# A decoder's expert stage on one Trainium2 core: three blocks made one, rows weighed before the gather, results added up in DRAM by the scatters

## The reference

```python
N, D_MODEL, D_FF, N_EXPERTS, TOP_K = 2048, 256, 512, 8, 2
xn = _layernorm(x, ln_gamma, ln_beta)
xf = xn.reshape(-1, D)
logits = jnp.clip(xf @ router_w.T, -CLAMP, CLAMP)
probs = ...                                   # softmax over 8 experts, clipped
topk_p, topk_i = jax.lax.top_k(probs, TOP_K)
dense_gate = zeros((N, N_EXPERTS)).at[arange(N)[:, None], topk_i].add(topk_p)
for eid in range(N_EXPERTS):
    xe = xf * dense_gate[:, eid:eid + 1]      # the gate weighs the input row
    gu = xe @ gate_up_w[eid].T
    gate, up = jnp.split(gu, 2, axis=-1)
    hidden = jax.nn.silu(gate) * up
    out = out + hidden @ down_w[eid].T
return x + out
# and around it: x = _layernorm(x + that)     -> layernorm(2 x + out)
```

## Time and profile before

| what | us |
|---|---|
| median of 3 runs (lowest, highest) | 1420.37 (1419.14, 1420.39) |
| the profiled execution, its time | 1422.48 |
| the profiled execution, its span | 1420.8 |
| expert stage in it: block 1 | from about 1076 to 1145 |
| block 2 | from 1145 to 1388 |
| block 3 | from 1388 to the end |

### The profile page before, as it was taken

How to read it: one execution, slowest core, us unless ns; L and a number is a source line. 1 busy time by engine, 2 the same in 40 slices (tenths; PEclk the granted TensorE clock), 3 DMA queues, 4 the chain that set the end, 5 groups by cost and what they waited for, 6 DMA issues and landing times. The chain is left out here.

```text
span 1420.8 us, 25057 instructions
## 1 busy us (share of the span) xinstructions
PE 1197.0 (84%) x8059; PEld 873.5 (61%) x8060; DVE 881.0 (62%) x1545; ACT 743.3 (52%) x2046; POOL 608.3 (43%) x664
## 2 busy tenths in 40 slices
PE   7888589575999999999899999998984368999970
PEld 4544367454667767776666777665763357777750
DVE  2588799773445555563445566665886656677745
ACT  2598457334556556655555566652661035555532
POOL 1155457557436223322633322101664336666635
PEclk9999799797899999999999999999996569999995
DMA  9100000010010010001010001005401001111105
GB/s 303 27 1 0 0 1 2 1 30 16 16 30 16 16 30 16 16 1 31 15 25 17 5 16 45 1 1 224 133 1 45 23 19 49 44 48 48 48 33 178
DMA packets 36136, 56.04 MB, mean 39 GB/s; under 512 B 6528, under 2 KB 27392, under 8 KB 36032
## 3 DMA queue, kind: packets, MB, share of 16 engines
q1 hardware_dynamic: 32288, 44.47, 10.5%
q0 software_dynamic: 3744, 10.23, 2.2%
HBM read 34.90 MB, written 9.31 MB: 31 GB/s over the span
## 5 line engine op out<-in xcount | busy, mean ns | idle before, releaser
L2016 DVE TENSOR_REDUCE ga_neg_top<-ps 128x1 f32<-128x128 f32 (+7 forms) x256 | 181.9, 752 | 195.2 <-PE ps L1786 194.8
L1897 ACT ACTIVATE ga_e<-ps,ga_neg_top 128x128 f32<-128x128 f32 (+7 forms) x256 | 188.2, 743 | 7.5 <-DVE ga_neg_top L2016 6.8
L1906 ACT COPY ga_e_tr<-ps 128x512 f32<-128x512 f32 (+3 forms) x192 | 92.0, 479 | 174.6 <-PE ps L1795 172.1
L1795 PE MATMUL ps<-ident,ga_e 128*128 128x128 f32 x1152 | 165.1, 279 | 0.8 <-DVE ga_e_tr L2024 0.8
L1811 PE MATMUL ps<-ga_e_tr,ga_v 128*64 128x256 f32 x1152 | 151.7, 391 | 4.1 <-ACT ga_att L1914 4.1
L1795 PEld LDWEIGHTS ps<-ident,ga_e 128*128 128x128 f32 x1152 | 123.3, 142 | 28.0 <-ACT ga_e L1897 14.7
L2024 DVE COPY ga_e_tr<-ps 128x128 f32<-128x128 f32 (+3 forms) x192 | 105.8, 551 | 35.1 <-PE ps L1795 34.8
L2528 DVE TENSOR_TENSOR ex_w_lo<-ex_gate_up,ex_w_hi 128x1024 fp32r<-128x1024 f32 x78 | 92.7, 1229 | 42.1 <-ACT ex_w_hi L2493 42.0
L1971 POOL TENSOR_TENSOR ga_q_lo<-shared,ga_q_hi 128x1024 fp32r<-128x1024 f32 x15 | 35.5, 2370 | 175.5 <-ACT ga_q_hi L1887 175.5
L2493 ACT CAST ex_w_hi<-ex_gate_up 128x1024 fp32r x78 | 77.9, 1046 | 50.5 <-PEq L2189 35.0
L1811 PEld LDWEIGHTS ps<-ga_e_tr,ga_v 128*64 128x64 f32 x1152 | 72.4, 136 | 48.9 <-issue 23.3
(11 more groups left out here) (330 smaller groups left out, 2738.7 us busy)
## 6 DMA issues: line engine op xcount, KB each, us to landing
shared<-shared SPq DMA_DIRECT2D x80, 128.0 KB, 2.4
ex_gate_up<-in_ex_gate_up SPq DMA_DIRECT2D x1, 8192.0 KB, 24.3
ex_down<-in_ex_down SPq DMA_DIRECT2D x1, 4096.0 KB, 35.7
x_tr<-in_x_tr SPq DMA_DIRECT2D x4, 512.0 KB, 7.3
x_nat<-in_x SPq DMA_DIRECT2D x1, 2048.0 KB, 11.7
xn_rows<-x_tr SPq DMA_DIRECT2D x8, 256.0 KB, 2.1
x_tr<-choice_rows SPq DMA_DIRECT2D x8, 256.0 KB, 4.9
shared<-choice_rows SPq DMA_DIRECT2D x8, 256.0 KB, 5.5
```

The costliest lines, as they stand in the source:

```text
L1795: last = nc.tensor.transpose(ps_tr[n % 2][:, (kb - k0) * P:(kb - k0 + 1) * P], e[half][t % 2][:, kb * P:(kb + 1) * P], core.ident[:])
L1897: nc.scalar.activation(e[half][t % 2][:, 0:blocks(t) * P], ps_scores(t, half), ACT.Exp, bias=neg_top[t % 2][:, half:half + 1], accum_out=s ...
L1906: nc.scalar.copy(e_tr[g % 2][:, k0:k1, half, t % 2 * P:(t % 2 + 1) * P], ps_tr[n % 2][:, 0:(k1 - k0) * P].rearrange("p (k t) -> p k t", t= ...
L2016: nc.vector.tensor_reduce(neg_top[t % 2][:, half:half + 1], ps_scores(t, half), AX.X, ALU.max, negate=True).then_inc(top_ready, 1)
```

## The change

The three blocks become one, and four things change within it.

1. **Rows are weighed in advance.** As soon as a choice's gates are known, ACT multiplies all 16 tiles of `xn` with them (L2410 of the changed kernel, 32 activations of 128x256), and SP writes them to `gated_rows` (16 DMAs of 256 KB, a row for each choice). `xn_rows` goes. The loop's gather fetches by the choice's number straight into `row`; POOL's multiplication and the buffer `tokens_in` go. The gather of a tile waits until PE has transposed the tile before it.
2. **The slot table** needs two bf16 numbers a slot and no gates: no work on POOL, `at_place` has room for both choices, the running sum over experts takes 3 steps in place of 8, and the expert of each slot tile is worked out after the one-hots.
3. **The scatters add.** They have `compute_op=ALU.add` and go to `summed_rows`, which has one row for each token and is filled with 2x beforehand: ACT doubles x in 4 activations of 128x1024 and SP writes them in 5 DMAs. POOL waits for the scatter before, ahead of each.
4. **The last part** loads one tensor (8 DMAs of 256 KB), and neither POOL's nor DVE's addition is left. SP waits for the scatters itself.

The core of the diff:

```diff
+                for n in range(TILES // DOUBLED):
+                    tiles = slice(n * DOUBLED, (n + 1) * DOUBLED)
+                    sp.wait_ge(doubled_ready, n + 1)
+                    sp.dma_start(summed_rows[0:N, :].rearrange("(n p) d -> p n d", p=P)[:, tiles, :],
+                                 doubled[n // len(HALVES)][:, HALVES[n % len(HALVES)], :]).then_inc(summed_written, 16)
+                sp.dma_start(summed_rows[N:N + P, :], doubled[0][:, 0, :]).then_inc(summed_written, 16)
+                for i in range(2):
+                    for g in range(GROUPS_OF_TILES):
+                        tiles = slice(g * GROUP, (g + 1) * GROUP)
+                        sp.wait_ge(gated_ready, i * GROUPS_OF_TILES + g + 1)
+                        sp.dma_start(gated_rows[i * N:(i + 1) * N, :].rearrange("(n p) d -> p n d", p=P)[:, tiles, :],
+                                     gated[i][:, tiles, :]).then_inc(gated_written, 16)
+
+                sp.wait_ge(scattered, 16 * SLOT_TILES)
...
+        def fetch(pool, g):
+
+            nc.gpsimd.tensor_copy(tile_source[:], column(source, g)).then_inc(source_ready, 1)
+            pool.wait_ge(source_ready, g + 1)
+            apart(pool, core.pool_waited)
+            nc.gpsimd.indirect_dma_start(row, None, gated_rows,
+                                         bass.IndirectOffsetOnAxis(ap=tile_source[:], axis=0)).then_inc(gathered, 16)
...
+                pool.wait_ge(gated_written, 16 * 2 * GROUPS_OF_TILES)
+                pool.wait_ge(sources_ready, 1)
+                fetch(pool, 0)
+
+                def step(g, t, u1, u2, u3):
+                    if g is not None and not at(g, 0):
+                        need(pool, rows_tr_ready, g)
+                        apart(pool, core.pool_waited)
+                        fetch(pool, g)
+                    if u3 is not None:
+                        pool.wait_ge(down_copied, u3 + 1)
+                        apart(pool, core.pool_waited)
+                        nc.gpsimd.tensor_copy(tile_target[:], column(target, u3)).then_inc(target_ready, 1)
+                        pool.wait_ge(target_ready, u3 + 1)
+                        need(pool, scattered, 16 * u3)
+                        apart(pool, core.pool_waited)
+                        nc.gpsimd.indirect_dma_start(summed_rows, bass.IndirectOffsetOnAxis(ap=tile_target[:], axis=0),
+                                                     rows_out, None, compute_op=ALU.add).then_inc(scattered, 16)
...
+                for i in range(2):
+                    act.wait_ge(gates_ready, i + 1)
+                    for t in range(TILES):
+                        last = nc.scalar.activation(gated[i][:, t, :], xn[:, t, :], ACT.Copy, scale=gates[:, i, t:t + 1])
+                        if t % GROUP == GROUP - 1:
+                            last.then_inc(gated_ready, 1)
+
+                act.wait_ge(sources_ready, 1)
+                act.wait_ge(gated_written, 16 * 2 * GROUPS_OF_TILES)
+                act.wait_ge(summed_written, 16 * (TILES // DOUBLED + 1))
```

More of the change, by code:

```diff
@@ L2104, in stage_experts @@
     BATCHED = BANK // D
+    LEFT = EXPERTS // 2
+    CHOICE_PARTS = 2
+    DOUBLED = 4
+    HALVES = [slice(n, n + DOUBLED) for n in range(0, TILES // 2, DOUBLED)]
     GROUPS_OF_TILES = TILES // GROUP
@@ L2271, in _ @@
                 last.then_inc(ranks_ready, 1)
+                pe.wait_ge(choice_values_ready, 1)
                 for i in range(2):
                     pe.wait_ge(places_ready, i + 1)
[L2275 to L2279, removed]
@@ L2282, in _ @@
+                lagged(pe, SLOT_TILES, 2, step, turns=True)
             @block.scalar
             def _(act):
+                act.wait_ge(core.x_loaded, 16)
+                for n in range(TILES // DOUBLED):
+                    tiles = slice(n * DOUBLED, (n + 1) * DOUBLED)
+                    nc.scalar.activation(doubled[n // len(HALVES)][:, HALVES[n % len(HALVES)], :], core.x_nat[:, tiles, :], ACT.Copy,
+                                         scale=2.0).then_inc(doubled_ready, 1)
                 for n in range(TILES // BATCHED):
@@ L2292, in _ @@
+                lagged(act, SLOT_TILES, 2, step, turns=True)
+                for g in range(GROUPS_OF_TILES):
+                    act.wait_ge(offset_ready, g + 1)
+                    for t in range(g * GROUP, (g + 1) * GROUP):
+                        last = nc.scalar.activation(xn[:, t, :], xn[:, t, :], ACT.Identity, bias=offset[:, t:t + 1],
+                                                    scale=rstd[:, t:t + 1])
+                    last.then_inc(final_ready, 1)
             @block.vector
@@ L2344, in _ @@
-                for x in range(1, EXPERTS):
-                    link(nc.vector.tensor_tensor(ends[:, x:x + 1], ends[:, x - 1:x], count[:, x:x + 1], ALU.add))
-                link(nc.vector.tensor_tensor(starts[:], ends[:], count[:], ALU.subtract))
+                link(nc.vector.tensor_copy(count, count_int[:]))
+                for n, distance in enumerate((1, 2, 4)):
+                    summed = reach[n + 1][:, LEFT:] if n < 2 else ends[:]
+                    link(nc.vector.tensor_tensor(summed, reach[n][:, LEFT:], reach[n][:, LEFT - distance:LEFT - distance + EXPERTS], ALU.add))
@@ new lines, in _ @@
+                link(nc.vector.tensor_tensor(starts[:], ends[:], count, ALU.subtract))
+                link(nc.vector.scalar_tensor_tensor(work[:], starts[:].unsqueeze(1).to_broadcast(by_tile), float(P), ps_rank[:, 0:TILES, :],
+                                                    ALU.mult, ALU.add))
+                link(nc.vector.tensor_tensor(picks[:], picks[:], work[:].unsqueeze(1).to_broadcast([P, 2, TILES, EXPERTS]), ALU.mult))
+                link(nc.vector.reduce_sum(slots_f[:], picks[:], AX.X))
@@ L2349, in _ @@
+                for i in range(2):
+                    one_hot(at_place[:, i * TILES:(i + 1) * TILES, :], place_f[:, i, :], place_iota, P).then_inc(places_ready, 1)
                 by_slot = [P, SLOT_COLUMNS, EXPERTS]
@@ L2371, in _ @@
-                link(nc.vector.tensor_copy(gate_parts[:, 0].bitcast(F32R), gates[:]))
-                link(nc.vector.tensor_tensor(gate_parts[:, 1], gates[:], gate_parts[:, 0], ALU.subtract))
-                for i in range(2):
-                    last = one_hot(in_tile[:, i], tile_f[:, i, :], slot_iota, SLOT_COLUMNS)
-                last.then_inc(in_tile_ready, 1)
-                link(nc.vector.tensor_scalar(slots_part[:], slots[:], P - 1, None, ALU.bitwise_and))
-                link(nc.vector.tensor_copy(place_f[:], slots_part[:]))
```

351 lines of the change are left out of this document (144 added, 207 removed).

## The result

The changed kernel takes 1496.81 us (median of 4 runs, 1493.11 to 1498.83), the kernel before, run beside it, 1420.38 (1419.14 to 1425.89). The ratio is 1.0527, with a 95% interval from 1.0492 to 1.0562. The predicted time was 1389.0, the range 1379 to 1416. The profiled executions have spans of 1491.3 and 1420.8 us, so 70.5 us have to be found in the traces.

What follows compares the result with a forecast made beforehand. POOL's full turn, mean 5.57 us, was taken as the loop's bound, with PE close behind. Front -12.9, loop -4.2, scatter to load -6.7 and last part -8.0 sum to -31.8 against 1420.8, a median of about 1389; range 1379 to 1416.

Steps and rivals of the forecast that it cites:

- POOL in the loop: POOL's turn without multiplication and gap: 5.49 to 4.55 us, nothing late behind the gather's new wait, POOL no longer the bound.
- the rival for the slower side: Loop: an adding scatter that lands late holds ACT; at d = 2.8 a turn takes 7.4, time 1460; chance 0.16.
- POOL's own turn: Loop: POOL's work per turn, 5.49 us less 0.94 for the multiplication and its gap, 4.55.
- The front: From the count to PE's first transposes: shorter slot table chain of 15.5 us, weighed rows hidden with almost no cover; gain 12.9.
- The adding scatter: Loop's scatter chain: 4.6 us plus d; with d = 0.8 a turn of 5.4, together -4.2 us.
- d: Extra time of an adding scatter over a plain one, bounded by 0 and 2.8 us, taken as 0.8.
- max(5.2, 4.6 + d): Loop turn: the larger of PE's 5.2 us and the scatter chain's 4.6 + d; 5.4 at d = 0.8.
- The two ends: After the last scatter: SP's load sooner, 6.7; last part 24.5 us (bounds 21.5 and 24.5, by POOL's DRAIN) for 32.5, 8.0.
- a group's 1.5: Last part: eight groups at 1.5 us each, 12.0 in all, where a group took 2.78 before.
- A small d: Loop rival: d under 0.5, PE the bound at 5.2 a turn, time 1381; chance 0.26.
- late weighed rows: Front rival: the 16 writes to `gated_rows` end 13.7 us after the sources, front's gain gone, time 1403; chance 0.08.
- The second rival: Loop: scatter's extra between 1.2 and 1.7; at 1.4 a turn takes 6.0, time 1410; chance 0.10.

Runs made afterwards that it cites:

- experiment 1: Changed kernel with the scatter placed ahead of the gather in POOL's step, all waits kept: 1389.41 us, ratio to the kernel before 0.9778.
- experiment 2: Changed kernel, old order, with two buffers for gathered rows, so the gather waits for PE's transposes of the tile before the last: 1393.56 us, ratio 0.9793.
- experiment 3: Kernel before with only one wait added: POOL's gather waits for PE's transposes of the tile before. 1505.2 us, ratio 1.0573.
- experiment 6: Changed kernel with the scatter ahead of the gather and two buffers for finished rows and their indices: 1383.68 us, ratio 0.973.
- experiment 5: Changed kernel with the scatter ahead of the gather and scatters that overwrite in place of adding (addition in DRAM left out): 1378.69 us, ratio 0.9701.
- experiment 7: Changed kernel, gather still ahead of scatter, with two buffers for gathered rows and two for finished rows: 1380.79 us, ratio 0.9711.
- experiment 8: Changed kernel with the scatter ahead of the gather, plus a POOL drain right behind the last scatter: 1387.23 us, ratio 0.9752.
- experiment 4: Changed kernel, order and waits kept, with scatters that overwrite in place of adding: 1467.1 us, ratio 1.0317.

## Why the prediction was wrong

**The step that failed** is in *POOL in the loop*: "Behind the new wait at the gather (PE's transposes of the tile before) nothing is late: copy, gap and landing are 3.9 us, and the next transposes come a turn, 5.2 us, later." That was reckoned for the gather, and for the gather it is right: PE waits for gathered rows 6.1 us in the whole changed kernel. What stands behind the waiting instruction on POOL is the scatter, and it was not reckoned. In POOL's step the gather of tile g goes with the scatter of tile g - 4. The wait is for PE's transposes of g - 1; the results of g - 4 have come from PE in the turn before that, so the scatter could go about when that turn begins, and the transposes come near its end (after the gate/up matmuls). The prediction priced the scatter's delay behind the wait at nothing, without a reason. The trace has 6.83 us from the data to the issue, and `rows_out` is single, so this goes once round the cycle. Experiments 1, 2 and 3 show the cause from three sides: order mended, wait mended, wait added alone. The prediction named the single buffer of the gather in its last line as what could make it wrong, but gave it no price and no chance; the rival for the slower side was put on the landing.

**POOL's own turn** is a second step that failed, hidden by the first. The prediction took 0.94 off 5.49, got 4.55 and went on with "So POOL isn't the bound any more". Without the chain through `rows_out` POOL's turn is 5.33 us (experiment 6): the scatter holds it 1.67 us in place of 1.52, and the copy behind it takes 0.77 in place of 0.18.

**The front** was right and too small. The -12.9 was reckoned to PE's first transposes; to the first gather's issue the same terms give 1134.8 - 1146.8 = -12.0, against -15.5. The count was there at 1115.7, 2.4 us sooner than before, and the chain behind it took 14.3 us in place of 15.5. ACT's 32 activations ended at 1123.6 and not at 1130.7, so the cover was wider than reckoned. `gated_rows` was there in time: POOL was released by the sources (27.9 <-DVE ex_source above), not by the writes.

**The adding scatter** landed as sized: 3.8 us. The prediction built this from a plain 3.0 and d = 0.8. In experiment 5 a plain scatter lands after 2.4 (median) in a loop just as busy, with an issue of 1.0. Against that one the addition costs 1.4, of which 0.6 is the issue; why the kernel before had 3.0 and 1.52 is not shown. So the landing is right by luck in part: no row gave d, and d is 0.8 or 1.4 by the plain scatter it is held against. By the turn's term, max(5.2, 4.6 + d), a turn should take 5.4; experiment 1 has 5.54, and experiment 7, with the chain opened, 5.22.

**The two ends** together: last scatter to the end 41.8 - 25.8 = 16.0, where 6.7 + 8.0 less 0.8 for the landing make 13.9. SP's first load starts 3.84 us after the issue (1469.33 after 1465.49), at once on landing. POOL's DRAIN has moved to the end and is exposed by 3 us, the upper of the two bounds and the one taken. The term that was too large is a group's 1.5: the groups are 1.21 apart.

**The other rivals.** That POOL's gap before the gather becomes a wait for PE was named as what the trace would show, and it does; what that wait does to the scatter was not. A small d is out (0.8 over the plain scatter of before, 1.4 over experiment 5's), and so are late weighed rows (first gather at 1131.3). The second rival's turn of 6.0 us at d = 1.4 did not come: it is 5.54 in experiment 1. The rival for the slower side had the sign right with another mechanism: it put 1460 on d = 2.8, a landing of 5.8 us, and the landing was 3.8.

**The whole**, with the failed step mended, is experiment 1, by the same three pieces:

| piece | predicted | experiment 1 | changed kernel |
|---|---|---|---|
| to the first gather | -12.0 | -15.0 | -15.5 |
| first gather to last scatter | -5.9 | -3.5 | +102.0 |
| last scatter to the end | -13.9 | -15.7 | -16.0 |
| sum | -31.8 | -34.2 | +70.5 |

(The middle term is 34 turns of -0.17, 0.8 for the last scatter but one, and 0.9 for the multiplication that the first tile no longer needs.) Experiment 1 takes 1389.41, where 1389.0 was predicted; that is no merit of the forecast, which was for the kernel as written, and it is luck in part even here. The middle piece agrees by two errors: from the first gather to the first scatter it fell from 24.0 to 18.2 us, for which the prediction had only the 0.9, and the 38 turns, which were to bring -5.8, rose from 208.2 to 210.5. And the medians differ by less than the spans: the profiled execution of the kernel before was 2.1 us above its median (1422.48, 1420.37), that of experiment 1 was 1.1 below (1388.33, 1389.41), so -34.2 in the spans is -31.0 in the medians.

## What to carry to other kernels

When an edit adds or moves a wait, list what is queued behind the waiting instruction on its own engine, with the tile that each entry belongs to, and ask for each how long its data has been ready by then. The check that the waiting instruction's own result is in time says nothing of those. A removed operation can also remove a buffer: `tokens_in` and its multiplication took 0.94 us of POOL's turn and bought a turn of slack, and a second `row` or another order had to replace it. And a fixed version should be compared piece by piece: here the total came out at the forecast with a loop that had gained nothing.

## What the runs showed of the hardware

- An adding indirect scatter of 128 rows of 1 KB lands 3.8 us after its issue begins, and the issue takes 1.60; the overwriting one has 2.4 and 1.0 (medians of experiments 1 and 5). Neither issue is a constant: the overwriting one took 1.53 in the kernel before, with 3.0 to landing, and the adding one 2.27 in experiment 6, where the next copy starts 1.67 us after it.
- POOL's drain after indirect DMAs took 6.4 to 6.7 us, 17 us after the last issue (changed kernel, experiment 1) as well as 2.6 us after it (kernel before); the next drain, with no indirect DMA in between, took 0.30 (experiment 8).
- In a loop that leaves PE idle for several us in every second turn, the granted clock fell: from 1.00 over the whole loop in experiment 1 to 0.83 from 1160 to 1450 us in the changed kernel, of which this is the row (busy us of PE, PEld, DVE, ACT, POOL, the clock, the DMA share, GB/s). The down matmuls, the same 312 in each kernel, took 460 ns each there and 380 in experiment 1. With overwriting scatters and turns of 7.5 us the granted clock was 0.94 (experiment 4, 1160 to 1430 us).

```profile
1160.00:1450.00 290.00, 223.19 (x889) 173.04 (x890) 136.57 (x171) 109.80 (x172) 103.09 (x135) 0.83 0.19 31
```

```profile
L2385 PE MATMUL ps<-ex_down,shared 128*128 x312 | 95.4, 460 | 48.4 <-ACT shared L2439 47.4
```

The Trainium skill (DMA: Bandwidth & Descriptors, Anatomy of one DMA) gives a DMA issued by POOL about 2.0 us and its bytes over 436 GB/s; for these 128 KB that makes an estimate of 2.3 us. The overwriting scatter's 2.4 agrees with it; the adding one's 3.8 lies 1.5 above.
